# Cross-attention and ternary FFN on one core: loads reordered, out-projection weights in pieces, one split moved ahead

## The chip, the cores and the metric

One Trainium2 chip, one core of it. The kernel is one launch; its inputs and its output lie in the device's memory (HBM). The metric is the device time of one execution in microseconds; lower is better. Engines in the text: PE (TensorE, matrix multiplies and transposes), DVE (VectorE), ACT (ScalarE), POOL (GpSimd) and SP (SyncE), which here only issues DMAs. Each works through its own list of instructions in order; semaphores hold an instruction until others are done.

## What is computed

`x` is 4 x 512 x 512, the context 4 x 512 x 256; 32 heads of 16. Cut to what matters:

```python
def attention(x, ctx, pos):                 # x comes in layer-normalised
    q = rope(x @ Wq, pos); k, v = split(ctx @ Wkv); k = rope(k, pos)
    w = softmax(einsum('bqhd,bkhd->bhqk', q, k) / 4)
    return einsum('bhqk,bkhd->bqhd', w, v).reshape(4, 512, 512) @ Wout + bout

def bitlinear(x, w):                        # layer_norm, absmax quantisation, ternary weights
    x_hat = absmax_quant(layer_norm(x))
    gamma = mean(abs(w))
    return einsum('bsd,od->bso', x_hat, sign(round(w / (gamma + 1e-6))) * gamma)

x = x + attention(layernorm(x), ctx, pos)
x = x + bitlinear(gelu(bitlinear(layernorm(x), w_fc)), w_proj)
```

## The kernel before

The program is written out by hand, one list for each engine, in three stages.

**Project** (16 tiles of 128 rows). PE turns the inputs (L240, L246), multiplies them with Wk, Wv and Wq (L256) and turns the rotated result back (L280). DVE takes the statistics of x (L348), normalises, and makes the rotary products (L367 to L369); POOL adds the products (L442). ACT copies and sums the absolute FFN weights for gamma (L424). SP loads context, x and FFN pieces (L195, L200, L217, L219) and, after every second tile, stores two tiles of q and k, each in three bf16 parts (`store_parts`, L230, 12 DMAs). A tile's x is in one of four slots.

**Attend** (32 groups: 4 batch entries times 8 groups of 4 heads). `load_stacks` (L526, seven DMAs a group, 768 KB) brings the parts of q and k back as stacked operands, into four slots; group g uses slot g % 4. `tensor_step(s)` on PE works on three groups at once: `scores` of group s (L599), whose maxima DVE takes (`row_maxima`, L669, two heads-and-chunks a time, with two score slots in PSUM); `scores_turned` of group s-2 (L625), with the maxima as two more rows of the stack; and the products with v (`weigh_v`, L638). The maxima's way from DVE to the stack is: POOL splits them in bf16 parts (`split_maxima`, L703 to L709), PE turns them (`turn_max`, L608), ACT copies them (`save_max`, L696), SP sends them into row 96 of the stack (`load_max`, L531). ACT makes the exponentials (L689). One FFN weight block a group is prepared beside it: `load_weight` (L538, L541), `ternarise` on POOL (L718 to L723; block n uses slot n % 2 and waits for gamma), `turn_weight` (L547). The sums of the softmax go out and back (`store_sums`, `load_sums`, `invert_sums` L675, `store_inverse`, `load_quotients` L573/L574), and POOL divides (L733).

**Rows** (16 tiles). `mix` (L853) multiplies with Wout, `add_residual` on DVE (L889) adds x plus bias (`add_bias` on POOL, L1002), ACT centres (`centre_u`, L981), DVE quantises, SP turns (`turn_u`, L825); `expand` (L867, 32 matmuls) and `contract` (L879, 32 matmuls) are the two FFN products. PE's order is expand(s), mix(s+2), contract(s-2).

On POOL the Attend loop reads, before the change:

```python
                if s < GROUPS:
                    att.ternarise(pool, s)
                    att.split_maxima(pool, s)
```

PE calls `turn_max(pe, s - 1)` inside `tensor_step(s)`, after the fourth of group s's eight scores. SP's list at the seam of Project and Attend is: tile stores, `load_stacks` 0 and 1, tile stores, `load_stacks` 2 and 3, then `load_weight` 0 and 1.

## Time and profile before

| | |
|---|---|
| median of 3 runs | 849.15 us (848.03 to 849.91) |
| the profiled execution | 848.58 us, its span 846.5 us |
| mean granted TensorE clock | 0.972 |
| PE busy | 784.4 us (93%) |
| DVE busy | 681.3 us (80%) |
| ACT busy | 454.3 us (54%) |
| POOL busy | 337.8 us (40%) |

The span runs from the first to the last instruction; the profiled execution's own time is 2.1 us longer. Busy shares are averages over three stages with different limits. A granted clock of 1.00 is 2.4 GHz, 0.50 is 1.2 GHz.

### The profile page before, as it was taken

The page shows a single profiled execution, that of the slowest core. Times are in us where ns is not written, and L with a number is a line of the kernel's source. Part 1 is how long each engine was busy: PE and PEld are TensorE (multiplying, and loading weights), DVE is VectorE, ACT ScalarE, POOL GpSimd, SP SyncE. Part 2 cuts the span into 40 slices and gives each one's busy share as a digit, 9 for nine tenths or more (in the row PEclk, how much of TensorE's full clock was granted, in tenths as well). Part 3 has the DMA queues.
Part 4 walks back from the last instruction along what each step waited for, and adds up shares of the span by engine and source line. Part 5 has one row for each costly group of instructions (what it writes and reads, how often), then busy time and mean ns, then how long its engine had stood idle before and what let it go on. Part 6 is the DMA issues. An engine that isn't in the chain of part 4 may idle for free.

```text
span 846.5 us, 11693 instructions
## 1 busy us (share of the span) xinstructions
PE 784.4 (93%) x3842; PEld 334.0 (39%) x3842; DVE 681.3 (80%) x937; ACT 454.3 (54%) x825; POOL 337.8 (40%) x428
## 2 busy tenths in 40 slices
PE   1999997499999999999999989887999999999995
PEld 0788885023223223222232222233444444444442
DVE  5888885588888888888888868157999899988883
ACT  4466664067777777777777757642322432233230
POOL 3688875364445544555444535312222111111000
PEclk9999998589999999999999989999999999999999
DMA  8288877634455555676655773224466535654463
GB/s 273 83 216 233 253 189 168 163 90 118 120 154 149 143 155 135 148 144 163 163 143 142 201 134 85 71 74 79 110 117 137 120 87 108 112 117 88 83 128 88
DMA packets 175579, 116.14 MB, mean 137 GB/s; under 512 B 116512, under 2 KB 147232, under 8 KB 175520
## 3 DMA queue, kind: packets, MB, share of 16 engines
q1 hardware_dynamic: 175520, 115.40, 56.1%
q8 instruction: 31, 0.51, 0.3%
q14 instruction: 28, 0.23, 0.1%
HBM read 64.50 MB, written 25.43 MB: 106 GB/s over the span
## 4 chain that ended last, share of the span: by engine, by line
PE 80%; DVE 7%; DMA 5%; SPq 3%; ACT 2%; issue 2%; POOL 1%; DVEq 0%; POOLq 0%; ACTq 0%
PE banks L638 15%; PE banks L625 14%; PE banks L599 12%; PE banks L879 11%; PE banks L867 10%; PE banks L256 9%; PE banks L853 5%; DMA stack_words<-max_rows 2%; PE banks L280 1%; SPq L230 1%; DVE h_scales L945 1%; SPq L526 1%; ACT probs_words L689 1%; PE banks L246 1%; DVE probs_words L954 1%
## 5 line engine op out<-in xcount | busy, mean ns | idle before, releaser
L669 DVE TENSOR_REDUCE maxima<-banks 128x2 f32<-128x1024 f32 x256 | 302.1, 1216 | 67.2 <-PE banks L599 67.1
L689 ACT ACTIVATE probs_words<-banks 128x512 f32<-128x512 f32 x512 | 276.3, 597 | 105.3 <-PE banks L625 103.5
L625 PE MATMUL banks<-stack_words 98*128 98x512 bf16 x512 | 175.7, 386 | 6.6 <-DMA stack_words<-max_rows 4.6
L599 PE MATMUL banks<-stack_words 96*128 96x512 bf16 x512 | 160.8, 397 | 9.1 <-DMA stack_words<-k_parts 4.8
L638 PE MATMUL banks<-probs_words,late_words 128*32 128x512 f32 x1024 | 137.2, 608 | 0.5
L867 PE MATMUL banks<-ternary_words,late_words 128*128 128x512 f16 x512 | 114.6, 382 | 8.1 <-DMA late_words<-late_words 8.1
L879 PE MATMUL banks<-ternary_words,stack_words 128*128 128x512 f16 x512 | 114.6, 383 | 5.4 <-DMA stack_words<-stack_words 5.4
L995 ACT ACTIVATE probs_words<-probs_words,h_moments 128x2048 f32<-128x2048 f32 x16 | 32.0, 2002 | 130.9 <-DVE h_moments L937 130.9
L625 PEld LDWEIGHTS banks<-stack_words 98*128 98x128 bf16 x512 | 39.4, 97 | 147.9 <-ACT probs_words L689 85.4
L599 PEld LDWEIGHTS banks<-stack_words 96*128 96x128 bf16 x512 | 50.0, 100 | 73.9 <-DVE maxima L669 12.3
L879 PEld LDWEIGHTS banks<-ternary_words,stack_words 128*128 128x128 f16 x512 | 50.3, 99 | 71.4 <-issue 15.3
L867 PEld LDWEIGHTS banks<-ternary_words,late_words 128*128 128x128 f16 x512 | 50.2, 99 | 71.5 <-DMA late_words<-late_words 10.4
L703 POOL TENSOR_SCALAR neg_max<-maxima 128x16 f32<-128x16 f32 x32 | 8.2, 258 | 170.3 <-DVE maxima L669 170.3
L989 ACT ACTIVATE probs_words<-banks,row_scale 128x512 f32<-128x512 f32 x64 | 43.6, 685 | 43.4 <-PE banks L867 43.4
L1018 POOL TENSOR_SCALAR h_powers<-h_moments 128x1 f32<-128x1 f32 x16 | 3.6, 223 | 155.3 <-DVE h_moments L937 155.2
L853 PE MATMUL banks<-v_words,attn_words 128*128 128x512 f32 x128 | 57.5, 592 | 0.0
L718 POOL TENSOR_SCALAR late_words<-late_words,limits 128x512 f16<-128x512 f32 x32 | 50.2, 1568 | 12.9 <-DMA late_words<-in_L_ffn_w_fc_dram 12.9
L720 POOL TENSOR_SCALAR late_words<-late_words,limits 128x512 f16<-128x512 f32 x32 | 50.1, 1566 | 0.0
L446 POOL TENSOR_TENSOR ternary_words<-attn_words,ternary_words 128x512 bf16<-128x512 f32 x32 | 37.5, 1170 | 27.2 <-ACT ternary_words L418 27.2
L932 DVE BATCH_NORM_STATS2 h_stats<-probs_words 128x6 f32<-128x512 f32 x64 | 39.8, 681 | 3.7 <-ACT probs_words L989 3.7
L442 POOL TENSOR_TENSOR attn_words<-attn_words 128x512 f32<-128x512 f32 x32 | 41.4, 1292 | 3.2 <-DVE attn_words L369 2.0
L638 PEld LDWEIGHTS banks<-probs_words,late_words 128*32 128x32 f32 x1024 | 20.2, 108 | 54.6 <-ACT probs_words L689 38.9
(123 smaller groups left out, 935.0 us busy)
## 6 DMA issues: line engine op xcount, KB each, us to landing
o_rows<-late_words SPq DMA_DIRECT2D x32, 256.0 KB, 2.7
k_parts<-ternary_words SPq DMA_DIRECT2D x48, 128.0 KB, 2.5
q_parts<-ternary_words SPq DMA_DIRECT2D x48, 128.0 KB, 2.4
stack_words<-q_parts SPq DMA_DIRECT2D x32, 192.0 KB, 2.9
stack_words<-k_parts SPq DMA_DIRECT2D x96, 64.0 KB, 2.7
stack_words<-k_parts SPq DMA_DIRECT2D x32, 192.0 KB, 2.8
attn_words<-in_x_dram SPq DMA_DIRECT2D x16, 256.0 KB, 4.1
probs_words<-in_L_ffn_w_fc_dram SPq DMA_DIRECT2D x16, 256.0 KB, 3.6
```

The lines of the kernel that those rows point to most:

```text
L256: mm = self.nc.tensor.matmul(out, lhs[a][:, slot, k * P:(k + 1) * P], rhs[b][:, k, :], start=(a + b + k == 0), stop=(a == 1 and k == count ...
L599: mm = self.nc.tensor.matmul(self.score_slot[j % 2][:, i], self.mem.q_stack[0:STACK, slot, head, c * P:(c + 1) * P], self.mem.k_stack[0:ST ...
L625: self.nc.tensor.matmul(self.mem.banks[:, self.ST_BANK[k]], self.mem.k_stack[0:STACK + 2, slot, head, c * P:(c + 1) * P], self.mem.q_stack ...
L638: mm = self.nc.tensor.matmul(self.pv_bank[32 * j:32 * j + 32], self.v_ones[:, g % 2, c, j, :], self.probs[:, c, j, :], start=(c == 0), sto ...
L669: dve.tensor_reduce(self.maxima[:, g % 2, 2 * j:2 * j + 2], self.score_slot[j % 2], AX.X, ALU.max).then_inc(self.scores_read, 1)
L689: act.activation(self.probs[:, c, head, :], self.mem.banks[:, self.ST_BANK[k]], ACT.Exp, scale=1 / math.sqrt(HEAD)).then_inc(self.exp_done, 1)
L718: pool.tensor_scalar(self.below[:], self.raw[:, w], limits[:, 1, w:w + 1], None, ALU.is_lt).then_inc(self.cut, 1)
L720: pool.tensor_scalar(self.ternary[:, w], self.raw[:, w], limits[:, 0, w:w + 1], None, ALU.is_gt).then_inc(self.cut, 1)
L853: mm = self.nc.tensor.matmul(self.y_bank[n % 2], att.attnT[:, n // CHUNKS * KX + k, c * P:(c + 1) * P], self.wout_sb[:, k, :], start=(k == ...
L867: mm = self.nc.tensor.matmul(self.fc_bank[o], self.uT[:, n % U_SLOTS, part * KX + k], self.fcT[:, k, o], start=(k + part == 0), stop=(k == ...
L879: mm = self.nc.tensor.matmul(self.proj_bank[r], self.hT[:, r, part, k], self.projT[:, k // 2, k % 2], start=(k + part == 0), stop=(part == ...
L989: act.activation(self.h[:, n % H_SLOTS, o * DIM:(o + 1) * DIM], self.fc_bank[o], ACT.Gelu, scale=self.row_scale[:, n % U_SLOTS]).then_inc( ...
```

## The change

Five groups of edits, all of them to the order of the lists:

1. SP: the stacks of groups 0 and 1 are loaded in the Project loop (steps 14 and 16), the raw weight blocks 0 and 1 as soon as the last tile of q is projected, ahead of the last tile stores.
2. SP: the bias is loaded in step 25 of the Attend loop, Wout in four pieces of 128 rows in steps 26 to 29, x of tiles 0 and 1 in steps 30 and 31; before, all of it went in step 28.
3. POOL: in step 0 the maxima are split before the first weight block is made ternary.
4. ACT: `centre_u(0)` stands behind the fourth exponential of the last group, not behind the last one.
5. POOL and DVE: `add_bias(2)` goes ahead of `spread_u(1)` and of the division of pair 13; that division goes into step 1 of the Rows loop; the last `invert_sums` goes one step later.

```diff
-    def load_weights(self, sp, wout, bout):
+    def load_bias(self, sp, bout):
         sp.wait_ge(self.att.v_staged, 3 * HG)
-        sp.dma_start(self.wout_sb, wout.rearrange("(k p) n -> p k n", p=P)).then_inc(self.wout_loaded, DMA)
         sp.dma_start(self.bout_sb, bout.rearrange("(a d) -> a d", a=1).to_broadcast([P, DIM])
                      ).then_inc(self.bout_loaded, DMA)
+
+    def load_weight(self, sp, wout, k):
+        sp.wait_ge(self.att.v_staged, 3 * HG)
+        sp.dma_start(self.wout_sb[:, k], wout[k * P:(k + 1) * P]).then_inc(self.wout_loaded, DMA)
...
         if n == 0:
-            pe.wait_ge(self.wout_loaded, DMA)
+            pe.wait_ge(self.wout_loaded, KX * DMA)
...
+                if s == TILES + 4:
+                    sp.wait_ge(prj.projected[1], TILES)
+                    att.load_weight(sp, w_fc, w_proj, 0)
+                    att.load_weight(sp, w_fc, w_proj, 1)
                 if within(s - 5, TILES) and (s - 5) % 2 == 1:
                     prj.store_parts(sp, s - 5)
-                if s >= TILES + 6 - STACK_SLOTS:
-                    att.load_stacks(sp, s - TILES - 6 + STACK_SLOTS)
+                if s in (14, 16):
+                    att.load_stacks(sp, s // 2 - 7)
+            att.load_stacks(sp, 2)
+            att.load_stacks(sp, 3)
 
             for s in range(GROUPS + 3):
-                if s < GROUPS:
+                if 2 <= s < GROUPS:
                     att.load_weight(sp, w_fc, w_proj, s)
...
-                if s == GROUPS - 4:
-                    rows.load_weights(sp, wout, bout)
-                    rows.load_x(sp, x, 0)
-                    rows.load_x(sp, x, 1)
+                if s == GROUPS - 7:
+                    rows.load_bias(sp, bout)
+                if GROUPS - 6 <= s < GROUPS - 2:
+                    rows.load_weight(sp, wout, s - GROUPS + 6)
+                if GROUPS - 2 <= s < GROUPS:
+                    rows.load_x(sp, x, s - GROUPS + 2)
...
-                if s == 1:
+                if s == 2:
                     att.invert_sums(dve, PAIRS - 1)
...
-                if s == GROUPS + 1:
-                    rows.centre_u(act, 0)
+                    if k == 3 and s == GROUPS + 1:
+                        rows.centre_u(act, 0)
...
+                if s == 0:
+                    att.split_maxima(pool, s)
                 if s < GROUPS:
                     att.ternarise(pool, s)
+                if 1 <= s < GROUPS:
                     att.split_maxima(pool, s)
...
             rows.spread_u(pool, 0)
+            rows.add_bias(pool, 2)
             rows.spread_u(pool, 1)
-            att.divide(pool, 13)
-            rows.add_bias(pool, 2)
...
-                if s in (3, 5):
-                    att.divide(pool, PAIRS - 2 + (s - 3) // 2)
+                if s in (1, 3, 5):
+                    att.divide(pool, PAIRS - 3 + s // 2)
```

SP's list around steps 14 and 15 of the Project loop, before (L230 stores q parts, L195 and L200 load context and x of tile 15, L217 and L219 an FFN piece):

```order
L230 DMA q_parts<-ternary_words 64x4x256 x4
L195 DMA attn_words<-in_ctx_dram 128x256
L200 DMA attn_words<-in_x_dram 128x512
L217 DMA probs_words<-in_L_ffn_w_fc_dram 128x512
L219 DMA probs_words<-in_L_ffn_w_proj_dram 128x512
```

and in the changed kernel:

```order
L230 DMA q_parts<-ternary_words 64x4x256 x4
L526 DMA stack_words<-q_parts 48x2048
L526 DMA stack_words<-q_parts 32x2048
L526 DMA stack_words<-q_parts 16x2048
L526 DMA stack_words<-k_parts 16x2048 x3
L526 DMA stack_words<-k_parts 48x2048
L195 DMA attn_words<-in_ctx_dram 128x256
L200 DMA attn_words<-in_x_dram 128x512
```

Seven DMAs of group 0's stack now stand ahead of the last loads of context and x.

SP's list at the end of step 28 of the Attend loop, before (L531 is `load_max`, L547 `turn_weight`, L813 and L814 Wout and bias, L819 x):

```order
L531 DMA stack_words<-max_rows 2x16x128
L547 DMA_TRANSPOSE ternary_words<-late_words 128x4x128
L813 DMA v_words<-in_L_xattn_Wout_dram 128x4x512
L814 DMA v_words<-in_L_xattn_bout_dram 128x512
L819 DMA v_words<-in_x_dram 128x512 x2
L541 DMA late_words<-in_L_ffn_w_proj_dram 128x2x256
```

and in the changed kernel, at the same place:

```order
L531 DMA stack_words<-max_rows 2x16x128
L547 DMA_TRANSPOSE ternary_words<-late_words 128x4x128
L818 DMA v_words<-in_L_xattn_Wout_dram 128x512
L541 DMA late_words<-in_L_ffn_w_proj_dram 128x2x256
L526 DMA stack_words<-q_parts 48x2048
```

Four DMAs (Wout whole, the bias, two tiles of x) have become one, a quarter of Wout; the others stand at the same place of steps 25 to 31.

POOL's list from the last division of the Attend loop on, before (L733 divides, L1002 adds the bias, L1008 and L1011 are `spread_u`, L1018 `spread_h`):

```order
L733 TENSOR_TENSOR attn_words<-late_words 128x512
L1008 TENSOR_SCALAR u_powers<-u_moments 128x1
L1011 TENSOR_TENSOR u_powers<-u_powers,half_power 128x1
L1008 TENSOR_SCALAR u_powers<-u_moments 128x1
L1011 TENSOR_TENSOR u_powers<-u_powers,half_power 128x1
L733 TENSOR_TENSOR attn_words<-late_words 128x512
L1002 TENSOR_TENSOR v_words<-v_words 128x512 x2
L1018 TENSOR_SCALAR h_powers<-h_moments 128x1
```

and in the changed kernel (the same lines are numbered three higher):

```order
L733 TENSOR_TENSOR attn_words<-late_words 128x512
L1011 TENSOR_SCALAR u_powers<-u_moments 128x1
L1014 TENSOR_TENSOR u_powers<-u_powers,half_power 128x1
L1005 TENSOR_TENSOR v_words<-v_words 128x512
L1011 TENSOR_SCALAR u_powers<-u_moments 128x1
L1014 TENSOR_TENSOR u_powers<-u_powers,half_power 128x1
L1005 TENSOR_TENSOR v_words<-v_words 128x512
L1021 TENSOR_SCALAR h_powers<-h_moments 128x1
```

The addition of tile 2's bias stands between the two `spread_u`, and no division stands between it and the start of the Rows loop.

## Rows read from the trace of the kernel before

**Rows 1.** The page's part 4, shares of the chain that ended last.

```profile
PE 80%; DVE 7%; DMA 5%; SPq 3%; ACT 2%; issue 2%; POOL 1%; DVEq 0%; POOLq 0%; ACTq 0%
```

**Rows 2.** Windows: length, busy PE PEld DVE ACT POOL, granted clock, DMA share, GB/s.

```profile
400.00:460.00 60.00, 60.00 (x337) 17.72 (x338) 51.76 (x51) 45.26 (x90) 32.03 (x40) 1.00 0.54 145
...
159.00:169.00 10.00, 1.22 (x5) 0.31 (x4) 1.79 (x2) 0.28 (x2) 5.80 (x8) 0.50 0.40 104
```

**Rows 3.** The chain from 118 to 176 us: start, us, what.

```profile
159.23 3.43 DMA late_words<-in_L_ffn_w_fc_dram
...
168.30 0.29 PE banks L608
...
173.04 0.43 PE banks L625
```

**Rows 4.** Timeline from 120 to 180 us: start, us, engine, line, tiles, [idle before].

```profile
136.06 1.08 PE L256 MATMUL banks<-wq_high,xT_low 128*128 128x512 f32 x4
...
141.92 1.04 PE L599 MATMUL banks<-stack_words 96*128 96x512 bf16 x2 [4.78 <-DMA stack_words<-k_parts]
...
156.06 4.72 DVE L669 TENSOR_REDUCE maxima<-banks 128x2 f32<-128x1024 f32 x4
```

**Rows 5.** Timeline from 104 to 124 us, of SP, DVE, POOL and PE.

```profile
107.12 0.43 SPq L200 DMA_DIRECT2D attn_words<-in_x_dram  x1
...
112.82 0.69 DVE L348 BATCH_NORM_STATS2 project_stats<-attn_words 128x6 f32<-128x512 f32 x1
...
115.16 1.29 POOL L442 TENSOR_TENSOR attn_words<-attn_words 128x512 f32<-128x512 f32 x1
...
117.09 0.60 PE L280 MATMUL banks<-ident,attn_words 128*128 128x128 f32 x4
```

**Rows 6.** Loads of x from 60 to 108 us, issue to landing.

```profile
DMA to landing us min/median/max: 2.9/4.2/5.8
```

**Rows 7.** The chain, from 336 to 374 and from 455 to 500 us.

```profile
365.36 6.01 DMA stack_words<-max_rows
...
482.38 9.08 DMA stack_words<-max_rows
```

**Rows 8.** Timeline of PE from 457 to 502 us.

```profile
470.08 0.23 PE L608 MATMUL banks<-identb,max_parts 128*32 128x128 bf16 x1
...
481.69 0.23 PE L608 MATMUL banks<-identb,max_parts 128*32 128x128 bf16 x1
...
491.51 0.61 PE L625 MATMUL banks<-stack_words 98*128 98x512 bf16 x1 [3.81 <-DMA stack_words<-max_rows]
...
499.64 0.23 PE L608 MATMUL banks<-identb,max_parts 128*32 128x128 bf16 x1
```

**Rows 9.** DMA issues from 400 to 460 us, then from 460 to 500 us.

```profile
late_words<-in_L_ffn_w_fc_dram SPq DMA_DIRECT2D x2, 256.0 KB, 2.8
...
v_words<-in_L_xattn_Wout_dram SPq DMA_DIRECT2D x1, 1024.0 KB, 5.5
```

**Rows 10.** Timeline from 536 to 600 us.

```profile
552.25 3.60 PE L853 MATMUL banks<-v_words,attn_words 128*128 128x512 f32 x8
...
553.21 0.72 ACT L981 ACTIVATE v_words<-late_words,u_moments 128x512 f32<-128x512 f32 x1
...
560.00 2.33 PE L867 MATMUL banks<-ternary_words,late_words 128*128 128x512 f16 x10 [3.15 <-DMA late_words<-late_words]
...
572.42 0.69 DVE L889 TENSOR_TENSOR late_words<-banks,v_words 128x512 f32<-128x512 f32 x1 [3.60 <-POOL v_words L1002]
...
585.76 8.51 PE L867 MATMUL banks<-ternary_words,late_words 128*128 128x512 f16 x32 [4.91 <-DMA late_words<-late_words]
...
590.57 0.35 DVE L675 RECIPROCAL sums<-sums 128x32 f32<-128x32 f32 x1 [3.13 <-DMA sums<-o_rows]
```

**Rows 11.** The chain, from 520 to 596 and from 590 to 620 us.

```profile
564.73 5.04 DMA late_words<-inverse_rows
...
604.61 6.91 PE banks L867 x32
```

## The prediction

> **What bounds the kernel now.** I read the page's part 4 first: 80% of the chain that ended last is PE, 5% DMA, 3% SP [rows 1]. Then the windows: in the middle of the Attend stage PE is busy 60.00 of 60 us at granted clock 1.00 (2.4 GHz), while the DMA engines are busy 0.54 of the time [rows 2]. A gain can only come from places where PE stands still, or works at 1.2 GHz because it stood still. The chain and the idle times in the timeline show three such places, and the change touches each.
>
> First, the seam of Project and Attend. PE ends the last q product at 136.06 + 1.08 = 137.14 and begins the first scores at 141.92, 4.78 idle behind a stack load [rows 4]. Then PE stops at `turn_max(0)` until 168.30, since POOL has the first ternary block ahead of the split and its raw weights land only at 159.23 + 3.43 = 162.66 [rows 3]. The first L625 stands at 173.04. From 159 to 169 PE is busy 1.22 us, at clock 0.50 (1.2 GHz) [rows 2].
>
> Second, 491.51: PE waited 3.81 us for the maxima's rows, whose load took 9.08 us [rows 7, 8]. From one `turn_max` to the next it is 481.69 - 470.08 = 11.61 us, and over this place 499.64 - 481.69 = 17.95, so it costs 6.34: 3.81 of wait and 2.5 of work at half clock behind it [rows 8].
>
> Third, the seam of Attend and Rows: PE is idle 3.15 before expand(0) at 560.00 and 4.91 before expand(2) at 585.76, which then takes 8.51 [rows 10] instead of 6.91 [rows 11].
>
> **The change part by part. First seam.** With stacks 0 and 1 in place the first scores start at 137.2. DVE has the last rotary products ahead of the first maxima, so I move the maxima by 4.3, not 4.78. Group 0's are done at 156.06 [rows 4] - 4.3 = 151.8. Group 1's eight follow without a stop, 4.72 / 4 = 1.18 each [rows 4]: done at 161.2. The last scores of group 1 start when six of them are done, 158.9, and end near 160. POOL has the raw weights by then (issued at 137.2, and 3.43 to land), so what followed their landing, 168.30 - 162.66 = 5.64 for ternary block and split together [rows 3], now starts at 151.8, split first: PE's turn finds the split done, and the block is ternary at 157.4. That counts because SP's `load_weight(2)` waits for it and `load_max(0)` is queued behind that. Two issues and a landing of some 3 us put the maxima in the stack at about 161. So the first L625 moves from 173.04 to 161.2: 11.8 gained.
>
> What SP pays: the seven DMAs of stack 0 go ahead of tile 15's x, issued at 107.12 [rows 5]. At some 0.47 an issue (estimate from its 0.43) that is 3.3 us, so 110.4. Landing takes 2.9 to 5.8, median 4.2 [rows 6]: 113.3 to 116.2, median 114.6. DVE takes its statistics at 112.82 without waiting today [rows 5], so it now stands 1.8 us. Queued behind them on DVE are tile 12's rotary products, which POOL adds at 115.16 + 1.29 = 116.45 for PE's turn at 117.09 [rows 5]: 0.64 of cover. PE loses 1.8 - 0.6 = 1.2 (0 to 2.8). Stack 1's seven issues pass only one FFN piece and tile stores; I cost them nothing, since the store's parts come at PE's pace; without that cover, 3.3 us. The two raw loads put 0.9 us of issue ahead of the last stores; nothing but stacks 2 and 3 waits for these, and they are wanted only after 160.
>
> The clock stays unknown. PE comes to its first unbroken stretch at half clock as before, and the work that it now does at 1.2 GHz may be more. The restart at 491.51 cost 2.5 us; I take 0.6 (bounds -1.5 to 2.5). **Sum of this seam: 11.8 - 1.2 - 0.6 = 10.0.**
>
> **Wout in pieces.** Wout, bias and two x tiles (1.8 MB) went between `turn_weight` of step 28 and the stacks of step 29, and step 29's maxima queued behind them. Now 256 KB go there in each of seven steps. PE wants the rows about 9.08 - 3.81 = 5.3 after their issue: a landing of 6.01 with nothing of Wout near it cost 0.7 [rows 7]. A 256 KB load lands in 2.8 us here [rows 9], and the issuing gap before the next stacks leaves it time at 0.54 busy. I count the whole 6.3 as gained (from 3.8, if another late landing is left, to 6.3).
>
> Against this stands a rule of the Trainium skill, "DMA: Bandwidth & Descriptors", section Bandwidth: copies should be batched to 1 MiB or more, and small ones are dear. By its fit of 2.0 us plus bytes over 436 GB/s four pieces would take 10.4 us of transfer against 4.4 for the whole (estimate by that page). The rows have 5.5 for the whole against 2.8 for one 256 KB load [rows 9], so the trace agrees that pieces cost more in sum, but nothing waits for Wout before `mix(0)`, some five groups later.
>
> **Second seam.** `centre_u(0)` now stands behind the fourth exponential of the last group, about 545.3, instead of at 553.21 [rows 10]. It costs ACT 0.7; its short pauses there hide most, and I take 0.2 for PE. expand(0) followed the end of that centring by 560.00 - 553.93 = 6.1, so u(0) is turned at 552, before PE wants it. PE's earlier work ended at 560.00 - 3.15 = 556.85, so expand(0) starts at 557.05. expand 6.91 [rows 11] and mix 3.5 (3.60 for its eight passes, pipelined [rows 10]) make 10.4: mix(2) ends at 567.5. `add_residual(2)` came at 572.42, behind POOL's bias [rows 10], which stood behind division 13 and so behind a DMA from 564.73 to 569.77 [rows 11]. With the bias moved up, it starts at 567.6, 4.85 earlier. What follows until expand(2) took 585.76 - 572.42 = 13.3 and is not touched: 580.9. PE is ready at 557.05 + 20.8 = 577.9, so 3.0 idle instead of 4.91. After 3.15 idle at 560.00 ten matmuls took 2.33, full clock [rows 10]; I take it that this one also keeps it: 8.51 - 6.91 = 1.6 more. The inversion moved one step takes a wait of 3.13 off DVE at 590.57 [rows 10]; without it, expand(3), before at 604.61 [rows 11], would be late by what PE gained. Division 13 is wanted only by the last four tiles. **Sum: 4.85 + 1.6 = 6.4.**
>
> Then PE's rows run unbroken, and all later work keeps its distances. **Total 10.0 + 6.3 + 6.4 = 22.7.** The profiled execution took 848.58 against a median of 849.15; 848.58 - 22.7 = 825.9, and between the two bases I say **826**.
>
> **The rivals.**
> - *Wout's pieces do not help*: the 9.08 landing has another cause, as the 6.01 one has [rows 7], and returns. Against it: the 1.8 MB right before it. 832.
> - *The first seam gives less*: x lands after 5.8, so PE loses 2.8, and 2.5 at half clock: 11.8 - 2.8 - 2.5 = 6.5 gained, 829.5. For it: in the Project stage seven more DMAs meet a queue that is never quiet.
> - *The second seam's wait turns into another*: the clock falls in the 3.0 us, and half of the 4.85 goes to ACT, whose table load and last centring stand ahead of the first GELU: 826 + 1.6 + 2.4 = 830.
> - *The change doesn't do what it says at the first seam*: scores wait for DVE's or ACT's last tile anyway, and only the POOL order counts for little. A gain of 0 there: 836.
> - *Slower*: each of seven steps now has a load ahead of its maxima. If each made PE wait 2.8 (the piece's landing [rows 9]) and lose 2.5 of clock, seven times 5.3 is 37, and 826 + 37 = 863. It decides from 22.7 / 7 = 3.2 us a step. Against it: 0.54 busy. By the Trainium skill's batching rule above, this is the side on which pieces err.
>
> **How the numbers follow.** Forecast 0.65 (823 to 829); Wout 0.10; first seam less 0.10; second seam 0.09; nothing at the first seam 0.03; slower 0.02; 0.01 for no net effect. The lower end takes no loss of x's load (1.2), full clock at once (2.1) and some more: 822. The upper end takes in the first three rivals: 832.5. Within 0.2% (1.7 us) is about what a measurement of this kernel cannot tell from no change. Faster 0.97, same 0.01, slower 0.02.
>
> **What the profile after would show.** Right: no idle PE at 137; a short wait of DVE for x near 113; the first L625 near 162; no wait of PE for the maxima's rows in steps 26 to 31, and 11.6 us between turns; expand(0) without a wait, about 3 us before expand(2) and its 32 matmuls in 6.9. Wrong, if: DVE's wait at x is over 3 us; a 6.3 us step remains around 480; the clock falls before expand(2); or `load_max(0)` lands clearly after the last scores of group 1.

## The result, and the profile after

The changed kernel takes **828.92 us** (median of 4 runs, 827.48 to 830.68) against 849.39 us for the kernel before on the same chip (848.03 to 849.91): ratio 0.976, 95% interval 0.974 to 0.979. The forecast was 826, range 822 to 832.5. The profiled execution took 829.01 us, its span is 826.9 us, 19.6 less than before, at a mean granted clock of 0.979.

From the page of the kernel after: busy time by engine, the chain that ended last, and two groups of matmuls (busy, mean ns, idle before and its releaser).

```profile
PE 782.2 (95%) x3842; PEld 333.4 (40%) x3842; DVE 683.7 (83%) x937; ACT 454.8 (55%) x825; POOL 337.3 (41%) x428
...
PE 72%; DVE 6%; ACT 1%; DMA 1%; issue 1%; POOL 1%; SPq 0%; DVEq 0%; POOLq 0%; ACTq 0%
...
L625 PE MATMUL banks<-stack_words 98*128 98x512 bf16 x512 | 174.9, 385 | 2.2 <-ACT probs_words L689 1.8
...
L870 PE MATMUL banks<-ternary_words,late_words 128*128 128x512 f16 x512 | 114.8, 383 | 4.2 <-DMA late_words<-late_words 4.1
```

PE does the same work in fewer microseconds of span. The shares of the chain can't be set beside [rows 1] as they stand: those of before add up to the whole span, while the chain of the kernel after reaches back only to 143.81 us, and its shares add up to 83%. From 145 us on, DMA has 31.1 us of the chain before (six pieces) and 9.95 after (three). L625 stands idle for 2.2 in all where it was 6.6; L870 (`expand`, L867 before) still waits 4.1 once.

**First seam.** The timeline of the kernel after, SP, DVE, POOL and PE between 106 and 172 us (start, us, engine, line, tiles, idle before and its releaser).

```profile
107.74 3.31 SPq L526 DMA_DIRECT2D stack_words<-k_parts  x4
...
111.56 0.42 SPq L200 DMA_DIRECT2D attn_words<-in_x_dram  x1
...
115.45 0.69 DVE L348 BATCH_NORM_STATS2 project_stats<-attn_words 128x6 f32<-128x512 f32 x1 [2.86 <-DMA attn_words<-in_x_dram]
...
119.01 0.96 PE L280 MATMUL banks<-ident,attn_words 128*128 128x128 f32 x4 [2.07 <-POOL attn_words L442]
...
139.61 1.08 PE L256 MATMUL banks<-wq_high,xT_low 128*128 128x512 f32 x4
140.53 0.60 PE L599 MATMUL banks<-stack_words 96*128 96x512 bf16 x2
...
158.00 0.29 PE L608 MATMUL banks<-identb,max_parts 128*32 128x128 bf16 x1
...
160.51 0.82 SPq L531 DMA_DIRECT2D stack_words<-max_rows  x1
...
162.96 0.58 PE L625 MATMUL banks<-stack_words 98*128 98x512 bf16 x1 [0.19 <-DMA stack_words<-max_rows]
...
169.59 0.23 PE L608 MATMUL banks<-identb,max_parts 128*32 128x128 bf16 x1
```

Read it against [rows 3 to 5]. The scores follow the last q product at once, where they stood 4.78 before. The turn of the first maxima comes at 158.00 instead of 168.30, and the first L625 at 162.96 instead of 172.84, 9.9 earlier (the 173.04 of [rows 3] is the chain's figure, which counts pipelined matmuls otherwise than a timeline). The cost stands at the top: x(15) is issued at 111.56, not 107.12, DVE waits 2.86 for it, PE 2.07, and q ends at 139.61 + 1.08 = 140.69, not 137.14: 3.55 late. Only 2.07 of that is the wait. The rest is the clock behind it, in the windows of the kernel after (length, busy time of PE, PEld, DVE, ACT and POOL, granted clock, DMA share, GB/s):

```profile
117.00:123.00 6.00, 3.99 (x13) 3.32 (x14) 4.98 (x11) 3.50 (x8) 4.81 (x5) 0.72 1.05 314
```

The mean of 0.72 over these 6 us means a part at 1.2 GHz; the same window of the kernel before has 1.00. Once the scores run, DVE with the maxima is the fullest engine here: from 142 to 158 it is busy 15.83 of 16 us, and PE 10.01 at a granted clock of 0.64.

**Wout.** The timeline of PE in the kernel after, its `turn_max` of the same two groups as 481.69 and 499.64 in [rows 8], and `mix(0)`.

```profile
471.45 0.23 PE L608 MATMUL banks<-identb,max_parts 128*32 128x128 bf16 x1
...
483.06 0.23 PE L608 MATMUL banks<-identb,max_parts 128*32 128x128 bf16 x1
...
522.26 3.60 PE L856 MATMUL banks<-v_words,attn_words 128*128 128x512 f32 x8
```

483.06 - 471.45 = 11.61, where the distance was 17.95: 6.34 gained. `mix(0)` begins at 522.26 instead of 538.84, 16.58 earlier. This sum has a third term that the change did not aim at. The second `turn_max` comes 9.32 earlier (169.59 instead of 178.91). In the kernel before, one step, from 364.67 to 377.20, takes 12.53 instead of 11.61, with a wait of PE of 0.75 for the load of 6.01 us at 365.36 [rows 7]; the kernel after has no such step, 0.92 less. 9.32 + 0.92 + 6.34 = 16.58.

**Second seam.** The timeline of the kernel after, PE, DVE and POOL between 540 and 575 us; expand(2) is the second row.

```profile
540.20 7.08 PE L870 MATMUL banks<-ternary_words,late_words 128*128 128x512 f16 x32
...
565.18 8.77 PE L870 MATMUL banks<-ternary_words,late_words 128*128 128x512 f16 x32 [4.12 <-DMA late_words<-late_words]
...
550.75 0.69 DVE L892 TENSOR_TENSOR late_words<-banks,v_words 128x512 f32<-128x512 f32 x1 [1.72 <-PE banks L856]
...
555.51 2.26 DVE L957 TENSOR_SCALAR probs_words<-probs_words,h_scales 128x2048 f32<-128x2048 f32 x1
...
554.19 1.26 POOL L1005 TENSOR_TENSOR v_words<-v_words 128x512 f32<-128x512 f32 x1 [0.89 <-DMA v_words<-in_x_dram]
555.41 1.27 POOL L733 TENSOR_TENSOR attn_words<-late_words 128x512 f32<-128x512 f32 x1
```

Against [rows 10]: expand(0) has no wait and comes 19.80 earlier (3.2 more than `mix(0)`), `add_residual(2)` 21.67 earlier (5.1 more). But expand(2) comes only 20.58 earlier (4.0 more), still waits 4.12, and its 32 matmuls take 8.77. One row explains 0.97 of the lost 1.1: the clip of h (L957) takes 2.26. The same clip in the kernel before, from the timeline of DVE:

```profile
577.10 1.29 DVE L954 TENSOR_SCALAR probs_words<-probs_words,h_scales 128x2048 f32<-128x2048 f32 x1
```

POOL's division (L733), which the change put there, begins 0.10 ahead of the clip.

### The profile page after: what moved, and what is told of

It is laid out like the page before. It is cut to its first block, busy times and chain, and to the rows that moved or that the text cites. A ratio compares the mean times of both kernels' runs of the same rounds, so it can differ in the third digit from the quotient of the medians.

```text
span 826.9 us, 11697 instructions
## 1 busy us (share of the span) xinstructions
PE 782.2 (95%) x3842; PEld 333.4 (40%) x3842; DVE 683.7 (83%) x937; ACT 454.8 (55%) x825; POOL 337.3 (41%) x428
## 4 chain that ended last, share of the span: by engine, by line
PE 72%; DVE 6%; ACT 1%; DMA 1%; issue 1%; POOL 1%; SPq 0%; DVEq 0%; POOLq 0%; ACTq 0%
PE banks L638 15%; PE banks L625 15%; PE banks L599 13%; PE banks L882 11%; PE banks L870 11%; PE banks L856 6%; DVE h_scales L948 1%; DVE maxima L669 1%; ACT probs_words L689 1%; DVE probs_words L957 1%; DVE h_stats L935 1%; PE banks L608 1%; DMA stack_words<-stack_words 1%; ACT probs_words L998 0%; DVE stack_words L963 0%
## 5 line engine op out<-in xcount | busy, mean ns | idle before, releaser
L625 PE MATMUL banks<-stack_words 98*128 98x512 bf16 x512 | 174.9, 385 | 2.2 <-ACT probs_words L689 1.8
L599 PE MATMUL banks<-stack_words 96*128 96x512 bf16 x512 | 159.0, 392 | 4.9 <-DVE maxima L669 4.4
L870 PE MATMUL banks<-ternary_words,late_words 128*128 128x512 f16 x512 | 114.8, 383 | 4.2 <-DMA late_words<-late_words 4.1
L625 PEld LDWEIGHTS banks<-stack_words 98*128 98x128 bf16 x512 | 39.4, 97 | 142.3 <-ACT probs_words L689 85.1
L870 PEld LDWEIGHTS banks<-ternary_words,late_words 128*128 128x128 f16 x512 | 50.3, 99 | 67.6 <-DMA late_words<-late_words 5.5
```

What stands on the lines that cost most here:

```text
L599: mm = self.nc.tensor.matmul(self.score_slot[j % 2][:, i], self.mem.q_stack[0:STACK, slot, head, c * P:(c + 1) * P], self.mem.k_stack[0:ST ...
L625: self.nc.tensor.matmul(self.mem.banks[:, self.ST_BANK[k]], self.mem.k_stack[0:STACK + 2, slot, head, c * P:(c + 1) * P], self.mem.q_stack ...
L870: mm = self.nc.tensor.matmul(self.fc_bank[o], self.uT[:, n % U_SLOTS, part * KX + k], self.fcT[:, k, o], start=(k + part == 0), stop=(k == ...
```

## The experiments

Spans are of the profiled execution; medians and ratios are against the kernel before on the same chip (850.42 us for experiments 1 to 4, 849.29 for 6 to 9, 849.94 for 5, 10 and 11). The runs of one edited kernel differ by 1.4 to 4.8 us among themselves, and the profile is of one of them, now a short one and now a long one. So a gain of 1 or 2 us is read from distances within a trace, and whether it is there in the time, from the medians.

### 1. Stack 0 behind x(15)

```diff
-                if s in (14, 16):
-                    att.load_stacks(sp, s // 2 - 7)
+                if s in (15, 16):
+                    att.load_stacks(sp, s - 15)
```

> The changed kernel with the stack of group 0 loaded one step later, behind the last loads of context and x (and one FFN piece). Theory A (tile 15's x lands late behind the seven stack loads, DVE waits 2.9, PE 2.1 and then works at half clock): the wait of DVE at L348 near 112 is gone, the last q product ends at 137.1 instead of 140.7, nothing else moves, span 3.5 lower, about 823.4 instead of 826.9, time about 825.4. Rival B (the DMA queue is full in that stage, so any place of the stack costs the same): a wait moves to another load or to the stores' landing, and the q product ends at 139 or later, span above 825.5.

Measured: 826.46 us, ratio 0.973 (0.971 to 0.974), span 823.8. The timeline of SP, DVE and PE in this kernel:

```profile
107.23 0.44 SPq L200 DMA_DIRECT2D attn_words<-in_x_dram  x1
...
112.92 0.69 DVE L348 BATCH_NORM_STATS2 project_stats<-attn_words 128x6 f32<-128x512 f32 x1
...
136.16 1.08 PE L256 MATMUL banks<-wq_high,xT_low 128*128 128x512 f32 x4
...
159.86 0.58 PE L625 MATMUL banks<-stack_words 98*128 98x512 bf16 x1 [0.54 <-DMA stack_words<-max_rows]
```

x(15) is back at 107.23, DVE doesn't wait, q ends at 137.24, the first L625 comes 3.10 earlier and the span is 3.1 shorter. The late x cost 3.1 to 3.5, not 1.2, and stack 0 didn't need to go ahead of it. The other profiles bear this out: with stack 0 ahead of x(15), q ends at 140.69, 139.40, 141.19 and 141.45 (the change and experiments 2, 5, 7), and with it behind, at 137.0 to 137.5 (1, 8, 9, 10, 11). The sure part of this is a wait of PE of 1.96 to 2.30. The fall of the clock behind it is not sure: in experiment 2 PE waited 1.96, the granted clock stayed at 1.00 from 117 to 123, and q ended 1.3 earlier than in the change.

### 2. Division 13 one step later

```diff
-                if s in (1, 3, 5):
+                if s in (2, 3, 5):
```

(with the pair's number worked out to suit; nothing else is changed from the kernel after)

> The changed kernel with POOL's division of pair 13 one step of the Rows loop later (2 instead of 1). Theory A (the clip L957 on DVE took 2.26 instead of 1.29 because POOL's division ran beside it): the clip takes 1.3 again, expand(2) starts 1.0 earlier relative to add_residual(2), PE's wait there is 3.1 instead of 4.1, and if the clock then holds its 32 matmuls take 6.9 instead of 8.8: span lower by 1.0 to 2.9. Rival B (the clip is slow for another reason, such as the SP or ACT reading the same tile): clip stays at 2.26, no gain. Rival C: the division later meets the next clip and what is won is lost again, span within 0.5 of 826.9.

Measured: 824.86 us, ratio 0.971 (0.968 to 0.974), span 826.0. `mix(0)` is at 522.27, as after. The timeline of DVE, POOL and PE in this kernel:

```profile
555.65 1.29 DVE L957 TENSOR_SCALAR probs_words<-probs_words,h_scales 128x2048 f32<-128x2048 f32 x1
570.83 2.18 DVE L957 TENSOR_SCALAR probs_words<-probs_words,h_scales 128x2048 f32<-128x2048 f32 x1
...
570.67 1.26 POOL L1005 TENSOR_TENSOR v_words<-v_words 128x512 f32<-128x512 f32 x1 [2.28 <-DMA v_words<-in_x_dram]
571.89 2.25 POOL L733 TENSOR_TENSOR attn_words<-late_words 128x512 f32<-128x512 f32 x1
...
564.32 8.77 PE L870 MATMUL banks<-ternary_words,late_words 128*128 128x512 f16 x32 [3.25 <-DMA late_words<-late_words]
```

The clip is back at 1.29 and expand(2) comes 0.86 earlier, with a wait of 3.25. The next clip now meets POOL instead: it starts 0.16 behind L1005 and takes 2.18, and L733 behind it takes 2.25 instead of 1.27. That one costs PE nothing. So the two instructions do not run at once: the later one stands until the earlier is done. The span is 0.9 shorter, all of it at the edited place. The median is 4.1 under that of the change; the trace doesn't show where the other 3 are, and it is of the longest of the four runs (the other three have spans of 821.5 to 823.0).

### 3. Wout in pieces alone

The kernel before with only the loads of Wout, the bias and x(0), x(1) spread as in the change.

```diff
-                if s == GROUPS - 4:
-                    rows.load_weights(sp, wout, bout)
...
+                if s == GROUPS - 7:
+                    rows.load_bias(sp, bout)
+                if GROUPS - 6 <= s < GROUPS - 2:
+                    rows.load_weight(sp, wout, s - GROUPS + 6)
```

> The kernel before with only Wout, bias and x of tiles 0 and 1 spread over steps 25 to 31. Theory A (the 1.8 MB ahead of step 29's maxima rows made the 3.81 wait): no wait of PE at 491, 11.61 from turn to turn, everything behind 6.3 earlier: span 840.2, time 842.3 (842 to 843). Rival B (another cause): a wait over 3 us returns in steps 26 to 31, span within 1 of 846.5. Rival C (the pieces are late in their turn, each 256 KB ahead of a step's maxima): several short waits of PE in L625, span above 843.

Measured: 842.58 us, ratio 0.992 (0.990 to 0.994), 7.8 under the kernel before by the medians; span 840.3, 6.2 under that of before. The timeline of PE in this kernel has one turn of 11.61 where 17.95 was:

```profile
480.72 0.23 PE L608 MATMUL banks<-identb,max_parts 128*32 128x128 bf16 x1
492.33 0.23 PE L608 MATMUL banks<-identb,max_parts 128*32 128x128 bf16 x1
```

The place itself gives 6.34. Of the span's difference another 1.0 was there before it (the turn at 480.72 instead of 481.69), and 1.1 was lost behind `mix(0)`: the matmuls of expand(0) took 9.90 behind a wait of 3.15, where they took 7.08 behind the same wait before. So that the span's 6.2 is so near to 6.3 is in part luck.

### 4. The split alone ahead

The kernel before with only POOL's order of step 0 changed.

```diff
+                if s == 0:
+                    att.split_maxima(pool, s)
                 if s < GROUPS:
                     att.ternarise(pool, s)
+                if 1 <= s < GROUPS:
                     att.split_maxima(pool, s)
```

> The kernel before with only the first split of the maxima ahead of the first ternary block on POOL. Theory A (the split's order alone frees PE's turn, but the maxima's rows still wait for the raw weights, since load_max(0) is behind load_weight(2), which waits for ternary block 0): turn_max(0) near 159.5 instead of 168.3, load_max(0) issued near 167.7 instead of 168.98, first L625 near 170.3 instead of 173.0: 2.7 gained, span 843.8. Rival B (the POOL order is what held the seam): first L625 before 166, 7 or more gained. Rival C (no gain at all, within 0.5 of 846.5).

Measured: 846.0 us, ratio 0.995 (0.993 to 0.997), span 844.9. The timeline of PE and SP in this kernel:

```profile
159.02 0.29 PE L608 MATMUL banks<-identb,max_parts 128*32 128x128 bf16 x1
169.91 0.59 PE L625 MATMUL banks<-stack_words 98*128 98x512 bf16 x1 [6.11 <-DMA stack_words<-max_rows]
...
166.60 0.34 SPq L538 DMA_DIRECT2D late_words<-in_L_ffn_w_fc_dram  x1
166.98 0.81 SPq L531 DMA_DIRECT2D stack_words<-max_rows  x1
```

The turn comes 9.3 earlier and yet the first L625 only 2.9 (172.84 before): SP holds `load_max(0)` behind `load_weight(2)` (L538), which waits for the first ternary block, and that waits for raw weights as late as before. The second `turn_max` comes 2.3 earlier and the span is 1.6 shorter; between them lie a late landing near 370 that costs 0.14 here instead of 0.92, the step of 17.95 [rows 8] that takes 18.85 here, and 0.5 lost behind `mix(0)`. The medians differ by 4.4, more than this trace accounts for.

### 5. The changed kernel without the split ahead

The edit of experiment 4 taken out of the kernel after.

> The changed kernel with one edit taken back: POOL ternarises weight 0 ahead of the split of the first maxima, as before. My theory: once the raw weight is loaded early and the thresholds stand at 148.6, POOL has the 4.5 of ternarising to fill its idle time up to the last maxima at 154.8, so the order no longer matters: first transposed score at 163.0 within 0.3, span 826.9 within 0.7. The two edits at this place are two ways to one gain and don't add up. Rival (the split must be ahead): the raw weight is there too late, the split ends 4.5 later and the first transposed score comes 3 to 4 later: span 830 to 831.

Measured: 828.51 us, ratio 0.973 (0.971 to 0.976): the same as the change. The timeline of POOL, SP and PE in this kernel:

```profile
149.46 1.59 POOL L718 TENSOR_SCALAR late_words<-late_words,limits 128x512 f16<-128x512 f32 x1 [0.46 <-POOL late_words L1283]
...
155.22 0.27 POOL L703 TENSOR_SCALAR neg_max<-maxima 128x16 f32<-128x16 f32 x1 [1.36 <-DVE maxima L669]
...
159.18 0.82 SPq L531 DMA_DIRECT2D stack_words<-max_rows  x1
...
163.07 0.63 PE L625 MATMUL banks<-stack_words 98*128 98x512 bf16 x1
```

With the raw weights early, the ternary block fits into POOL's idle time ahead of the last maxima, and the split still waits 1.36 for DVE. The first L625 is 0.1 later than in the change, though q ended 0.5 later here. The edit of POOL's order brings nothing that the medians show once the loads are early. The span is 828.1; the 1.2 over the change stands at `mix(0)` (523.51): 0.7 of it at the second `turn_max` (170.27 instead of 169.59), and 0.6 in two later steps of the Attend loop that take 11.80 and 11.99 instead of 11.61, where the edit changes nothing. What loads alone do is not separated further: no run has the raw weights early and the stacks late, or the other way round.

### 6. The edits behind the Attend loop alone

The kernel before with groups 4 and 5 of the change.

> The kernel before with only the edits behind the attention loop: the centring of tile 0 moved into the exponentials, the bias of tile 2 ahead of the second spread, division 13 and the last inversion moved into the tile loop. My theory: the first mix stands where it stood (538.8), the first expand comes some 3.1 earlier than 560.00 because its u is centred earlier, the add of tile 2 some 4.9 earlier than 572.42, and expand(2) only 3.8 earlier than 585.76, since the clip of h beside the moved division takes 2.3 instead of 1.29. Span 846.5 - 3.8 = 842.7, ratio about 0.9955. Rival (the sizes of the prediction on record, no slowed clip): expand(2) 4.85 earlier and its clock kept, 6.4 in all, span 840.1. Rival (the wait at the inversion was covered by something else as well): expand(2) where it was, span within 1 of 846.5.

Measured: 844.74 us, ratio 0.995 (0.993 to 0.997), span 843.5. The timeline of PE and DVE in this kernel:

```profile
557.08 7.08 PE L867 MATMUL banks<-ternary_words,late_words 128*128 128x512 f16 x32
...
581.75 8.77 PE L867 MATMUL banks<-ternary_words,late_words 128*128 128x512 f16 x32 [3.83 <-DMA late_words<-late_words]
...
567.63 0.69 DVE L889 TENSOR_TENSOR late_words<-banks,v_words 128x512 f32<-128x512 f32 x1 [1.72 <-PE banks L853]
...
572.13 2.26 DVE L954 TENSOR_SCALAR probs_words<-probs_words,h_scales 128x2048 f32<-128x2048 f32 x1
```

2.9, 4.8 and 4.0 earlier than before, the clip at 2.26 and the matmuls at 8.77: the same picture as in the whole change, without its first two parts. The span is 3.0 shorter (4.6 by the medians), and from `mix(0)` to the end it is 304.4 us against 307.7 before and 304.6 in the change.

### 7. The changed kernel with the centring late

```diff
-                    if k == 3 and s == GROUPS + 1:
-                        rows.centre_u(act, 0)
+                if s == GROUPS + 1:
+                    rows.centre_u(act, 0)
```

> The changed kernel with one edit taken back: the centring of tile 0 stands behind the last exponential again. My theory: the waits of expand(0) and of expand(2) are two links of one chain (DVE adds tile 2 only after mix(2), which stands behind expand(0)), so what expand(0) loses, expand(2) loses too: expand(0) near 543.3 with a wait of some 3, the add of tile 2 near 553.8, expand(2) near 568.3 with its wait still about 4; span 826.9 + 3.1 = 830.0, ratio to before about 0.9805. Rival (two separate waits, the later one absorbs the first): expand(2) stays within 0.5 of 565.2 with a wait of only 1, and the span stays near 827.

Measured: 835.61 us, ratio 0.984 (0.981 to 0.987), span 832.6. The timeline of PE in this kernel:

```profile
544.93 8.45 PE L870 MATMUL banks<-ternary_words,late_words 128*128 128x512 f16 x32 [3.16 <-DMA late_words<-late_words]
...
571.23 8.77 PE L870 MATMUL banks<-ternary_words,late_words 128*128 128x512 f16 x32 [4.08 <-DMA late_words<-late_words]
```

`mix(0)` is at 523.77 here, 1.5 later than in the change. Counted from it, expand(0) comes 3.2 later and expand(2) 4.5, with the same wait of 4.08. So the two waits are links of one chain, as expected, and do not absorb each other. The 1.3 more is the clock: behind the new wait of 3.16, expand(0) takes 8.45 instead of 7.08.

### 8. u(2) ahead of the clip of h(0), and 9. the same in all steps

Both from the kernel after with the edits of experiments 1 and 2. In step 1 of the tile loop (8), or in steps 1 to 14 (9):

```diff
+                if 1 <= s <= 1:
+                    rows.quantise_u(dve, s + 1)
                 if within(s - 1, TILES):
                     rows.clip_h(dve, s - 1)
-                if s + 1 < TILES:
+                if (s < 1 or s > 1) and s + 1 < TILES:
                     rows.quantise_u(dve, s + 1)
```

and in the same way `turn_u(s + 1)` ahead of `turn_h(s - 1, 0)` on SP.

> The changed kernel with stack 0 issued behind x(15) (as in the first experiment, 3.1 off the span), division 13 one step later, and in step 1 of the tile loop alone u of tile 2 quantised and turned ahead of the clip of h of tile 0, on DVE and on SP. DVE reaches u(2) about 1.4 after its add's statistics and then needs 3.0, the transpose lands 3.2 later: near 557 against the 558 at which mix(2) ends here, so expand(2) has no wait and its clock does not fall (7.07 instead of 8.77). Theory A (the wait causes the fall of the clock, and h of tile 0 has slack until its contraction 16 us later): expand(2) 4.1 earlier and 1.7 shorter than in the change; part of the 5.8 comes back as a wait of some 3 at expand(3), whose u stands behind the clip of h(1) as before. Span 826.9 - 3.1 - 2.5 = 821.3. Theory B (the clock falls at this place without a wait too): expand(2) still 8.8, span about 823. Rival C (h(0) late stops the first contraction): span no better than 823.8, with a wait at the contraction of tile 0.

> As the kernel ahead of it, but u of the next tile goes ahead of the clip of h in all steps from 1 to 14. Theory A: no wait at expand(2) nor at expand(3), the clock stays up: span 826.9 - 3.1 - 5.8 = 818.0. DVE waits some 1.4 in each step for the centring on ACT (its step is 16 us of work against 17.7 on PE), so it no longer gains on PE from step to step, and the rival is that h comes late from some step on: waits at the contractions, a longer last contraction's wait than the 5.45 now, and a span of 820 to 826.

Measured, 8: 826.13 us, ratio 0.974 (0.972 to 0.976), span 823.2. 9: 829.9 us, ratio 0.978 (0.977 to 0.980), span 827.8. The timeline of PE in experiment 8:

```profile
559.84 7.07 PE L870 MATMUL banks<-ternary_words,late_words 128*128 128x512 f16 x32
...
580.84 7.08 PE L870 MATMUL banks<-ternary_words,late_words 128*128 128x512 f16 x32 [3.59 <-DMA late_words<-late_words]
```

and in experiment 9:

```profile
576.06 7.08 PE L870 MATMUL banks<-ternary_words,late_words 128*128 128x512 f16 x32 [0.40 <-DMA late_words<-late_words]
...
734.62 7.08 PE L870 MATMUL banks<-ternary_words,late_words 128*128 128x512 f16 x32 [0.24 <-DMA late_words<-late_words]
752.31 7.08 PE L870 MATMUL banks<-ternary_words,late_words 128*128 128x512 f16 x32 [0.27 <-DMA late_words<-late_words]
...
817.46 7.07 PE L882 MATMUL banks<-ternary_words,stack_words 128*128 128x512 f16 x32 [3.53 <-DMA stack_words<-stack_words]
```

In 8 the wait at expand(2) is gone and its matmuls take 7.07, as theory A says, and a wait of 3.59 stands at expand(3). The span is 1.9 above theory A's, since `mix(0)` stands at 521.21 here, 1.7 later than in experiment 1; from `mix(0)` to the end it is 302.0 against 304.6 in the change, 2.6 less, as theory A has it. The time doesn't confirm a gain by this edit: the median is 2.4 above that of experiment 10, which differs by this edit alone, and the profile is of its shortest run. In 9 that one is gone too (0.40), but the rival came true, and more than it said (a span of 827.8, not 820 to 826): a tile now takes 752.31 - 734.62 = 17.7 instead of 17.3 of unbroken PE work, PE waits a little in most steps, and 5.36 and 3.53 ahead of the last two contractions, the first of which takes 9.02. From expand(3) to the end it is 251.7, against 242.8 in the change. In the change DVE waited for PE's contractions in these steps (7.6 in six waits between 650 and 750 us); in 9 it waits for ACT's centring instead (5.3 in six waits) and is busy 55.1 of the 60 us from 710 to 770 (54.4 in the change). So the waits follow DVE's list: u first in one step moved the wait to the next tile, and u first in each step made DVE and its wait for ACT the bound.

### 10. Both mended places

The kernel after with the edits of experiments 1 and 2 together.

> The changed kernel with the two mended places alone: stack 0 behind x(15), and division 13 one step later. If the two gains are separate (3.1 at the first seam, 0.9 at expand(2)), span 826.9 - 4.0 = 822.9 with a wait of 3.2 at expand(2) and 8.8 for its matmuls. If the later wait depends on how much the attention loop is ahead, the 0.9 is not there and the span is 823.8.

Measured: **823.72 us**, ratio 0.969 (0.967 to 0.971), span 823.6: the best of all by the median, 5.2 under the change, though its interval overlaps those of experiments 2 and 11. expand(2) from the timeline of PE in this kernel:

```profile
561.99 8.77 PE L870 MATMUL banks<-ternary_words,late_words 128*128 128x512 f16 x32 [3.13 <-DMA late_words<-late_words]
```

The wait is 3.13, 1.0 less than in the change, as expected. The span of the profiled execution is 0.7 above the sum, since `mix(0)` is at 520.07 here and at 519.53 in experiment 1.

### 11. mix(2) ahead of expand(0)

The kernel of experiment 10 with, on PE:

```diff
+            rows.mix(pe, 2)
+
             for s in range(TILES + 2):
...
-                if s + 2 < TILES:
+                if 3 <= s + 2 < TILES:
```

and the add, the centring, the quantising and the turn of u(2) moved up into step 0 on DVE, ACT, POOL and SP.

> As the two mended places, and mix(2) moved ahead of expand(0), with the add, the centring, the quantising and the turn of u(2) moved up behind it, into time in which DVE waited before (7.1 ahead of the add of tile 1, 1.7 ahead of that of tile 2). expand(2) then has no wait (u(2) is turned near 551.5, wanted at 558.2) and its clock stays up. What is left is the work that DVE still has behind: the clip of h(0) starts near 553, u(3) is done near 575.3 and turned near 578.5, while PE wants it at 575.6: a wait of some 2.9 at expand(3). expand(3) near 578.5 against 581.1, span 823.8 - 2.6 = 821.2. Rival (DVE's backlog is the whole cause and doesn't shrink): expand(3) at 581 as in the others, span 823 to 824, the waits only change their place. Rival on the other side: mix(2) ahead of expand(0) takes 3.5 from the start of h(0), and nothing is won back: span 826.

Measured: 824.44 us, ratio 0.970 (0.968 to 0.973), span 823.1. The timeline of PE and DVE in this kernel:

```profile
560.42 7.07 PE L870 MATMUL banks<-ternary_words,late_words 128*128 128x512 f16 x32
...
580.40 7.08 PE L870 MATMUL banks<-ternary_words,late_words 128*128 128x512 f16 x32 [2.57 <-DMA late_words<-late_words]
...
570.54 2.24 DVE L957 TENSOR_SCALAR probs_words<-probs_words,h_scales 128x2048 f32<-128x2048 f32 x1
```

expand(2) has no wait and a wait of 2.57 is left at expand(3). From `mix(0)` (521.70) to the end this kernel takes 823.1 - 521.70 = 301.4, against 303.5 in experiment 10, so of the forecast's 2.6, 2.1 is there. But `mix(0)` stands 1.6 later than in experiment 10 although nothing ahead of it differs, and the medians don't tell the two apart. So the span of 823.1 fits the rival's 823 to 824, and only the distances speak for the forecast: expand(3) comes 58.7 behind `mix(0)`, in experiment 10 60.9.

## Why the prediction was right, and where it was off

The direction, the three places and the total were right; the time came out 2.9 above the forecast, at the upper end of the likeliest case's own range. In spans, 22.7 was forecast and 19.6 came: 9.3 at the first seam, 6.3 at Wout, 3.0 behind `mix(0)`, and 0.9 from a late landing near 370 us of the kernel before that the kernel after doesn't have. The last is luck: the sum has no term for it, "all later work keeps its distances", and seven of the nine profiles with early loads have one to three such steps. Of the four signs of being wrong one appeared, the fall of the clock at expand(2), and DVE's wait for x, 2.86, missed its bound of 3 by little (3.09 in experiment 7).

- **Wout's pieces, 6.3.** Right to 0.1 (17.95 to 11.61), here and in experiment 3. The fear that pieces ahead of each step's maxima would stop PE seven times did not come true: turn to turn is 11.61 up to 506. The 10.4 against 4.4 us of transfer are estimates from a fit that the Trainium skill, "DMA: Bandwidth & Descriptors", states in its section Anatomy of one DMA, and for DMAs that GpSimd issues; these are issued by SP, so it need not hold for them. Nothing in the sum goes by it.
- **First seam, 10.0.** Near in sum (9.9 at the first L625, 9.3 at the next `turn_max`, which is what the later work got), but by luck, from two errors that nearly cancel. The 0.6 between the two places, where the granted clock is 0.67 (163 to 169; before, 0.78 from 173 to 179), is the size that the clock's term of 0.6 had. The term "PE loses 1.2" for the late x(15) was mis-sized: 3.55. The seven loads of stack 0 took 4.8 to issue where 3.3 was counted (the four of k 3.31, where those of stack 1 take 1.81), x was issued 1.2 later than I worked out, DVE took it 0.9 later (115.45 against 114.6), and behind PE's wait of 2.07 the clock fell, for another 1.5 (it did not behind 1.96 in experiment 2). Experiment 1 took all of it back. Against that, from the end of q to the first L625 it went from 35.7 to 22.3, where the forecast had 161.2 - 137.1 = 24.1, so 1.8 better: the maxima were done 13.9 behind q instead of 14.7, and their rows landed in 2.3, not "some 3".
- **Split and raw loads as one step.** I counted both edits as needed. Experiment 5 shows that with the stacks and the raw weights early the split need not go ahead, and experiment 4 that the split alone gets 2.9 at the first L625.
- **Second seam, 4.85 + 1.6.** It gave 3.0 behind `mix(0)` (19.6 - 16.6). "What follows until expand(2) took 13.3 and is not touched" is the step that failed: the same edit that moved division 13 put it beside the clip of h, and 13.3 became 14.4 (1.0 of it the clip). The second failed step is the clock: I took it that expand(2) would keep full clock behind 3.0 of idle, from the one row at 560.00. It waited 4.12, and took 8.77; it also took 8.77 behind 3.25 and 3.13 (experiments 2 and 10). So the 1.6 didn't come, and 0.3 was lost. The 1.6 was also too big by itself: it sets 8.51 of a timeline against 6.91 of the chain, and the timeline's figure for 32 matmuls at full clock is 7.08, so 1.4 was to be had. The last contraction, 9.37 where it took 8.69, has the other 0.7.

What stays open: spans of kernels that are alike up to `mix(0)` (experiments 1, 8, 9, 10, 11) have it at 519.5 to 521.7. The second `turn_max` stands at 166.2 to 167.8 in them, and the rest comes from one or two steps of the Attend loop between 340 and 390 us that take 11.8 to 12.6 instead of 11.61. What makes such a step in one profile and not in another no run shows. A difference of 1 to 2 us between two single profiles is therefore no evidence for an edit; the readings above go by distances within one trace, and where the medians don't confirm them (experiments 8 and 11) no gain in time is shown.

## What to carry to other kernels

Put an early load into a queue behind the load that is wanted next, and count the issues: seven DMAs ahead of one cost 2.3 to 4.3 us of PE's time here, about 2 of it a wait, and none behind it. Of two edits that remove the same wait, try each alone; one may be enough. A piece of work that is moved into "idle time" of one engine must be set against what its neighbour does in the same microsecond, and when an engine has a backlog, look where the wait goes when you reorder its list: here it went to the next tile, or to the end.

## What the runs showed of the hardware

**The clip on DVE and POOL's `tensor_tensor` stand still for each other.** A 128x2048 f32 `tensor_scalar` on DVE takes 1.29 us alone and 2.26, 2.18, 2.26, 2.24 when a 128x512 f32 `tensor_tensor` on POOL began just ahead of it. The later the clip starts behind POOL's instruction, the less it takes: 2.35 at a lag of 0.00 (586.33 in experiment 10), 2.26 at 0.10, 2.24 at 0.12, 2.18 at 0.16. Lag and duration add up to 2.34 to 2.36 each time, as if the clip did nothing until POOL was nearly done; had it only run slower beside POOL, its time would fall by less than the lag grows. POOL's, behind the clip, takes 2.25 instead of 1.27. The `tensor_reduce` ahead of the clip (L948) does not stretch: 2.25 in the change, with the first 0.4 of L1005 in it, and 2.25 before. The Trainium skill says this in "SBUF — State Buffer", section Who interferes with whom: a DVE instruction in its two-port mode and a GpSimd instruction exclude each other, and the one that starts second is blocked to the end of the first. By this rule the clip at 555.51 would end 1.29 behind POOL's 556.68, at 557.97; it ended at 557.77, so the trace agrees to 0.2. In which mode the clip ran, no row shows.

**The granted clock behind a wait.** The 32 matmuls of an expand take 7.08 at 2.4 GHz. Behind waits of 4.12, 3.25, 3.16 and 3.13 us they took 8.77, 8.77, 8.45 and 8.77, with part of the stretch at 1.2 GHz (granted clock 0.83 from 565 to 575 in the kernel after); behind 3.15 (before, expand(0)), 3.59 (experiment 8) and 2.57 (experiment 11) they took 7.08. In the last two the wait stands behind the first contraction, not behind a mix. But one place has it both ways: at expand(0), behind the same mix, 7.08 behind 3.15 (before), 9.90 behind 3.15 (experiment 3) and 8.45 behind 3.16 (experiment 7); and so has the wait for x near 119 us, with a clock of 0.72 behind 2.07 (the change) and 1.00 behind 1.96 (experiment 2). Neither the length of the wait nor the place decides it, and no run here settles what does.
